# A decoder layer on one core: two key tiles per row in the cross-attention loop, four score banks and a ring of three

## What is computed

```
x = x + self_attention(layernorm(x))              # 2 heads of 64, causal, rotary
Q = split_heads(layernorm(x) @ Wq + bq)           # 16 heads of 8
K = split_heads(ctx @ Wk + bk); V = split_heads(ctx @ Wv + bv)
attn = softmax(einsum('bhqd,bhkd->bhqk', Q, K) / sqrt(8))     # 256 x 1601 for each of 4 x 16 heads
x = x + merge(einsum('bhqk,bhkd->bhqd', attn, V)) @ Wo + bo
x = x + ffn(layernorm(x))                         # 128 -> 512 -> 128, gelu, low-rank terms
```

## Time and profile before

| | us |
|---|---|
| median of 3 runs | 388.24 |
| lowest and highest | 386.75, 391.52 |
| the profiled execution | 389.76 |
| its span in the profile | 387.9 |
| PE busy of the span | 353.2 (91%) |
| DVE busy | 296.4 (76%) |
| ACT busy | 295.7 (76%) |

### The profile page before, as it was taken

How to read it: one execution, slowest core, us unless ns; L and a number is a source line. 1 busy time by engine, 2 the same in 40 slices (tenths; PEclk the granted TensorE clock), 3 DMA queues, 4 the chain that set the end, 5 groups by cost and what they waited for, 6 DMA issues and landing times.

```text
span 387.9 us, 11520 instructions
## 1 busy us (share of the span) xinstructions
PE 353.2 (91%) x4652; PEld 162.6 (42%) x4652; DVE 296.4 (76%) x598; ACT 295.7 (76%) x592; POOL 133.6 (34%) x203
## 2 busy tenths in 40 slices
PE   8866979999999999999998999999989999799976
PEld 3342233444454434444543535443434444253334
DVE  3473888769999998699997897999958889671022
ACT  1432226888989789899899799898987998969923
POOL 8721580369410104899300106373000037000010
PEclk9999795899999999999999999999989999899999
DMA  7356378003552201135300220113002220000000
GB/s 287 125 161 188 106 237 282 21 2 130 188 159 66 72 11 65 57 129 187 131 6 2 85 79 9 52 49 135 13 2 74 88 59 4 0 17 1 2 2 15
DMA packets 19995, 31.95 MB, mean 82 GB/s; under 512 B 1444, under 2 KB 17486, under 8 KB 19942
## 3 DMA queue, kind: packets, MB, share of 16 engines
q1 hardware_dynamic: 19942, 31.21, 25.2%
HBM read 19.25 MB, written 11.96 MB: 80 GB/s over the span
## 4 chain that ended last, share of the span: by engine, by line
PE 58%; DVE 13%; ACT 12%; POOL 8%; issue 5%; DMA 3%; SPq 0%; ACTq 0%; DVEq 0%; POOLq 0%
PE wsum L1057 19%; PE score L1071 13%; PE ring L1027 10%; DVE part_max L719 9%; PE ring L1092 7%; ACT probs L910 6%; POOL k_parts L566 3%; PE score L1021 2%; DMA k_unit<-k_rows 2%; POOL k_rest L607 2%; POOL k_parts L612 2%; ACT q_unit L921 2%; ACT prob_self L941 1%; PE ring L1117 1%; PE ring L1148 1%
## 5 line engine op out<-in xcount | busy, mean ns | idle before, releaser
L719 DVE TENSOR_REDUCE part_max<-ring 128x1 f32<-128x512 f32 x384 | 239.3, 681 | 33.6 <-PE ring L1092 32.0
L910 ACT ACTIVATE probs<-score 128x512 f32<-128x512 f32 (+1 forms) x416 | 222.7, 597 | 32.7 <-PE score L1071 29.4
L1071 PE MATMUL score<-q_unit,k_unit 51*128 51x256 bf16 (+1 forms) x832 | 131.0, 279 | 8.6 <-ACT probs L910 6.5
L1057 PE MATMUL wsum<-probs,v_aug 128*32 128x256 f32 (+1 forms) x1664 | 136.2, 396 | 2.7 <-ACT unit_ctx L915 2.6
L1092 PE MATMUL ring<-k_unit,q_unit 51*128 51x512 bf16 x384 | 123.6, 400 | 3.9 <-DMA k_unit<-k_rows 2.3
L1071 PEld LDWEIGHTS score<-q_unit,k_unit 51*128 51x128 bf16 (+1 forms) x832 | 49.7, 97 | 106.1 <-ACT probs L910 61.7
L1057 PEld LDWEIGHTS wsum<-probs,v_aug 128*32 128x32 f32 (+1 forms) x1664 | 38.7, 109 | 40.2 <-issue 21.6
L566 POOL TENSOR_TENSOR max_parts<-neg_max,c_sb 128x8 bf16<-128x8 f32 x16 | 3.4, 210 | 120.4 <-DVE neg_max L727 120.4
L1092 PEld LDWEIGHTS ring<-k_unit,q_unit 51*128 51x128 bf16 x384 | 35.5, 95 | 15.8 <-DVE part_max L719 5.7
L646 POOL TENSOR_SCALAR prob_norm<-prob_self,prob_rsum 128x128 f32<-128x128 f32 (+1 forms) x12 | 9.0, 765 | 41.6 <-DVE prob_rsum L803 41.6
L921 ACT ACTIVATE q_unit<-ring 3x512 bf16<-3x512 bf16 x32 | 18.6, 580 | 4.9 <-PE ring L1109 4.7
(11 more groups left out here) (117 smaller groups left out, 318.7 us busy)
## 6 DMA issues: line engine op xcount, KB each, us to landing
k_unit<-k_rows SPq DMA_DIRECT2D x32, 300.2 KB
ctx_sb<-ctx_t SPq DMA_DIRECT2D x4, 800.5 KB, 9.7
k_rows<-k_parts SPq DMA_DIRECT2D x3, 601.5 KB, 3.4
k_rows<-k_parts SPq DMA_DIRECT2D x3, 599.2 KB, 3.3
even<-ffn_rows SPq DMA_DIRECT2D x3, 512.0 KB, 3.9
q_unit<-q_rows SPq DMA_DIRECT2D x30, 48.0 KB
k_rows<-k_parts SPq DMA_DIRECT2D x3, 401.0 KB, 4.2
k_rows<-k_parts SPq DMA_DIRECT2D x3, 399.5 KB, 4.1
```

The source lines that it names most:

```text
L719: v_.tensor_reduce(part_max[:, par, q, head, hp, c:c + 1], ring[s][:, 0:MW], AX.X, ALU.max)\
L910: a_.activation(probs[0:rows, i % PB, :], score[i % EB][0:rows, :], ACT.Exp)\
L1057: last = mm(wsum[32 * j:32 * j + 32, 0:S], v_aug[0:rows, v // UB % 3, at:at + 32], probs[0:rows, i % PB, S * (j // 2):S * (j // 2 + 1)], s ...
L1071: last = mm(score[i % EB][0:keys, S * hp:S * (hp + 1)], k_unit[rows, u, L * hp + P * t:L * hp + P * t + keys], q_unit[rows, u, hp, :], sta ...
```

## The change

Three edits. The score banks go from three to four and the ring from four to three. Scores and maxima of two key tiles, an even `g` and the odd one after it, stand in one row; the side work of the first is held back behind the row; then follow the two PVs that are due, `g - 4` and `g - 3`. Where the first tile carries `h0`, `h1` or `out`, or is the last of a unit, its side work is put directly behind it, and PV comes after the second tile all the same. How many maxima a tile has is as it was.

```diff
-EB = 3
+EB = 4
-NR = 4
+NR = 3
...
+LONG = ("h0", "h1", "out")
...
-    plan = []
+    plan, held = [], []
...
         plan += now
-        if t == 4 and v:
-            plan.append(("norm", v - 1))
+        side = [("norm", v - 1)] if t == 4 and v else []
         if t == TURN_AT[u] and v + 1 < UNITS:
-            plan.append(("mT", v + 1))
-        for *what, off in (SIDE if b < B - 1 else SIDE_LAST).get((u, t), []):
-            if 0 <= b + off < B:
-                plan.append((*what, b + off))
-        if t >= 3:
-            plan.append(("PV", v, t - 3))
-        elif v:
-            plan.append(("PV", v - 1, KT - 3 + t))
-    assert not todo
+            side.append(("mT", v + 1))
+        side += [(*what, b + off) for *what, off in (SIDE if b < B - 1 else SIDE_LAST).get((u, t), []) if 0 <= b + off < B]
+        g = KT * v + t
+        if g % 2 == 0 and t < KT - 1 and not any(item[1] in LONG for item in side):
+            held = side
+            continue
+        plan += held + side
+        held = []
+        if g % 2:
+            plan += [("PV", *divmod(i, KT)) for i in (g - 4, g - 3) if i >= 0]
+    assert not todo and not held
```

## The result

| | before | after |
|---|---|---|
| time, us, median (range) | 388.85 (386.75 to 392.54) | 432.43 (429.37 to 436.87) |
| profiled execution, us | 389.8 | 436.9 |
| PE busy in its span | 91% | 85% |

The changed kernel takes 1.117 times as long, with a 95% interval of 1.111 to 1.124: 43.6 us more. Forecast were 405 us, 17 more, and a range up to 416. The sign came out; the size lies outside the range. The profiled execution of after lies 4.4 us above its median, with a mean granted clock of 0.936, and that of before 1.0 above its own, with 0.965; so the 47 us between the two profiles are some 3 more than the medians give.

A forecast was written before the change was run, and what follows sets the result against it. PE, taking its work in program order, was taken to bound most of the loop, DVE close behind. -23 + 40 - 14 + 5 + 5 + 2 + 2 = +17 us, giving 405 us against the median; range 393 to 416.

The forecast's parts named there:

- The two small terms in the side work's blocks, +7: DVE's side work longer than PE's part of it, +5 us; ACT busy around `h0` and `h1`, +2 us.
- the ring's, at +40: Rows with three ring banks: fourth and fifth maxima wait on PE for DVE's reductions of the same row, +40 us.
- the part on ACT: Around `h0` and `h1`, table loads and gelus keep ACT; the wait begins one item earlier, three times, +2 us.
- 15 rows with three go free: Rows with three maxima were taken to wait for no ring bank, so they added nothing to the +40 us.
- The copy's wait: At seven odd unit borders, ACT's copy of `wsum` stands between two adjacent PVs: 0.71 us each, +5 us.
- The term -14: PE's present idle time, partly scores waiting for ACT, taken as all given back by a fourth score bank: -14 us.
- Ahead of the units: Unit 0's maxima alternate with projections, paced by DVE; one bank fewer costs +2 us, between 0 and 4.
- The last stage: It has a bank free each time, so the change costs 0 there.
- the -23: Fewer mode changes on PE between scores and PVs: 89 rows at 0.11 and 93 PV pairs at 0.14, -23 us.
- the drains are what counts: Faster rival: the fourth maximum doesn't wait, only savings stay: 365 us, or 379 if PE's present waits stay; chance 0.06.
- Worse: the ring couples three engines: Rival: side work takes ring banks, so next rows' first maxima wait for ACT, no wait given back: 420 us; chance 0.10.
- The no-change rival: DVE's pace was in the time already, so the gates fall mostly on time PE already lost: 391 us; chance 0.16.

The follow-up runs named there:

- the 64-column pair: After's and before's kernels, each large maximum's reduction reading 64 of its 512 columns: 385.41 us (ratio 0.999) and 385.3 us (ratio 0.996).

## Why the prediction was wrong in size

**Right.** The bound and its place: PE's order, held by DVE's reductions through the ring. The gate of 1.16 us for a fourth maximum (1.17 and 1.18 seen), a row of 1.47 (1.49), one of five at 2.07 (2.09), a pair of PVs at 1.00 (1.00). ACT's and DVE's busy times as before, PE's share down, waits for `probs` down. PVs: forecast -13 for the mode changes and +5 for the borders, measured -6.0. The two small terms in the side work's blocks, +7, came to +3.3 there.

**The step that failed** is the ring's, at +40. It counted a wait for each maximum beyond the third and let the side work behind the row pass free. In the part on ACT the sentence even stands, "With three banks the wait begins one item earlier"; I applied it to the three `h0` and `h1` places and not to the side work behind 56 rows. It should have been: the ring item behind n full maxima waits for reduction n - 2. That gives 1.16 behind three (1.37 seen), 0.42 + 0.68 + 0.60 + 0.06 = 1.76 behind four (1.86 seen) and 2.36 behind five (2.52 seen). By this rule 44 rows cost 27 x 0.29 + 11 x 0.30 + 6 x 0.29 = 13 us more, the eleven with short maxima about 3, and the forecast would have been 421 us. With the lengths as measured it is 24 more and 429; the 0.1 to 0.2 by which such rows are longer than the rule I haven't followed up. The forecast's own fifth maximum, 0.60 behind the fourth, was the pattern for it. The "15 rows with three go free" of the same paragraph fell with it: 11 of those rows have side work behind them. Nor is the rule the whole of it. It counts within a row, and the run with the banks alone lost 18.7 us in rows of a tile; and what is taken away ahead of the side work isn't simply gained, as the run with PVs ahead of it showed, since the bank must be back for the next row too.

**The borders.** The copy's wait was forecast at 0.71 each, 5 us; mending it gave 7.2. The wait for `mT`'s turn at the same borders wasn't in the sum; mending it gave 425.2 - 418.8 = 6.4 more (4.7 by the ratios). That the mended sum (429) comes near the measured 432 without it is partly luck: another term is too high by about as much, or this wait overlaps with what the rows' sums hold. I can't tell the two apart from these runs.

**The term -14** stands up within a few us, but only by difference: in the rows -10 (mode changes), +40 and +24 make 54, and 43.7 were measured, so 10 are missing, which before lost there (its tiles of three maxima have a median of 0.96 ahead of PVs, not 0.76, and its 132 tiles of two come to 86.4 us, 15 above 132 x 0.54). **Ahead of the units** the two profiles differ by 4.7 us, forecast 2; by the other kernels the bank costs about 2 and the term stands; the rest belongs to after's one execution, whose clock was low there. The last stage got 0.9, forecast 0.

**The savings.** Of the -23 the PVs' part is real on PE: pairs at 1.00. The 13 us less busy time in the 64-column pair is as much as 93 x 0.14, though that figure isn't split by kind of row. The rows' part of 10 can't be seen whole: with 64 columns rows of four have a median of 1.03 for the forecast 0.97, but there the fourth maximum's own wait (0.42 + 0.22 + 0.06 + 0.31 = 1.01) stands in the way. In the time the saving is worth little. With DVE's wait gone, both orders take 385, since ACT's waits at borders and at banks that it reads take the savings' place; with the borders mended at most 6.3 us show. So the rival "the drains are what counts" had its price wrong too: 365 to 379 us were given where 385 was measured.

**The rivals.** "Worse: the ring couples three engines" was nearest, at 420 with a chance of 0.10. Its argument (side work takes ring banks too) was the right one, with the wrong reader: what is late is mostly DVE's reduction ahead of the side work, not ACT's read behind it. The no-change rival fell with the half reductions in before, which changed its time by 2.5 us: no large part of its time was DVE's pace.

What stays open: whether an order that also takes ACT's waits for `q_unit` and `hidden` away would bring the rest of the saved busy time into the time; no such kernel was run.

## What to carry to other kernels

A rotating pool of banks is sized by the longest run of its items on the producing engine up to the next work that takes none of them, and the item that follows a row belongs to the row, whatever it computes. Count the items, not the kind that you are thinking of, and give each the release of the bank n places before it. Grouping work to save changes of mode lengthens exactly these runs: with a fixed sum of banks, compare 0.14 and 0.11 us saved for each row with 0.50 lost for the first item beyond the pool (1.49 in place of 0.97) and about 0.4 for each further one (1.86, with side work as the fifth item), before anything else. A row within the pool is not enough by itself: the banks must be back when the next row begins.

## What the runs showed of the hardware

A maximum over 512, 256 and 64 columns of PSUM took DVE 682 (or 681), 418 and 223 ns in mean of 384. The first step is 1.03 ns for a column (264 / 256), the second 1.02 (195 / 192), so a reduction is 1.02 ns a column and about 0.16 us besides. The Trainium skill (VectorE: DVE Perf Modes, The TRN2 errata) gives a PSUM source 120 cycles and one for each column at 0.96 GHz, which is 658, 392 and 192 ns: the slope agrees, the fixed part is measured 24 to 31 ns longer, and the measurement decides. Four in a row keep a pace of 0.60 us, 0.08 below the length of one. I had not expected the waits' own cost to be so steady: a bank freed by DVE was used by PE 0.06 us later in before and, with 1.17 = 0.42 + 0.68 + 0.07, in after too.
